# GpSimd's side jobs in the attention phase: weight sums put behind a unit's first row maxima, head sums and the power step behind the scales of every second or fourth unit

## The chip, the cores and the metric

The kernel runs on one core of one Trainium2 chip. The metric is the device time of one execution in microseconds (us). The five engines are TensorE (PE, with PEld for its weight loads), VectorE (DVE), ScalarE (ACT), GpSimd (POOL) and SyncE (SP), which here issues nearly all DMAs.

## The reference

Eight sequences of 100 latents and 361 context rows, width 1024, pass through one gated cross-attention block and one gated mixture of low-rank experts. Cut to what matters:

```python
def _L0_xattn_ref(latents, context, Wq, Wk, Wv, Wo, q_norm_w, k_norm_w):
    kv = jnp.concatenate([context, latents], axis=1)
    q = (latents @ Wq).reshape(bsz, q_len, HEADS, HEAD_DIM).transpose(0, 2, 1, 3)      # 32 heads of 128
    k = (kv @ Wk).reshape(bsz, kv_len, KV_HEADS, HEAD_DIM).transpose(0, 2, 1, 3)       # 8 KV heads
    v = (kv @ Wv).reshape(bsz, kv_len, KV_HEADS, HEAD_DIM).transpose(0, 2, 1, 3)
    q, k = rms_norm(q, q_norm_w), rms_norm(k, k_norm_w)
    scores = jnp.einsum('bhgqd,bhkd->bhgqk', q.reshape(bsz, KV_HEADS, groups, q_len, HEAD_DIM), k) * scale
    probs = jax.nn.softmax(scores.astype(jnp.float32), axis=-1)
    out = jnp.einsum('bhgqk,bhkd->bhgqd', probs, v)
    return out.transpose(...).reshape(bsz, q_len, HEADS * HEAD_DIM) @ Wo

x = x + tanh(g_xattn) * _L0_xattn_ref(layernorm(x), ctx, ...)
x = x + tanh(g_ffn) * experts(layernorm(x))        # top 2 of 8 experts of rank 16
```

## The kernel before

Every product of fp32 data is made of three fp32r matmuls (high by high, high by low, low by high). ScalarE makes a high part by a rounding copy, and VectorE makes the low part by a subtraction. The large products (keys and values, and the output projection) use seven block products in place of eight, which needs sums and differences of blocks of the weights and of the operands.

The execution has four stages: keys and values (up to about 682 us of the span), the attention of 64 units (682 to some 1441 us), the rest of the output projection, and the experts, which are partly woven into it.

**Units.** A unit u is one KV head g = u // 8 with one sequence b = u % 8, and holds R = 4 query heads. The instruction order of each engine is written out by hand in a function `slot(u)`, one for each engine. In slot u TensorE makes the four scores of unit u (`scores(u, i)`), then transposes and multiplies the probabilities of unit u - 1 (`turn_probs`, `values`), and between them makes a part of the query product for later units (`query_part`, until unit 55). I call a slot the time from TensorE's first matmul of `scores(u, 0)` (line 973, bank<-kT,q_hi) to that of unit u + 1.

**The softmax of head i of unit u.** VectorE takes the row maxima `mx` from the PSUM bank (L1923), then `nm` = -mx * rq (L1929, two operands in SBUF). ScalarE makes the exponential `pr` (L1539) with its row sum. VectorE takes the reciprocal `rr` (L1938). POOL scales `pr` by `rr` (`scale`, L901); the four scales of a unit release `turn_probs(u, 0)`. VectorE's order in a slot is: mx(0), nm(0), the low part of the previous unit's transposed probabilities `pT_lo(0)` (L1917), the query copy (L1875), mx(1), nm(1), rr(0), pT_lo(1), rr(1), mx(2), nm(2), pT_lo(2), rr(2), mx(3), nm(3), pT_lo(3), rr(3), every fourth mean square, then the next unit's `q_lo` (L1897), and in every odd slot up to 51 the low part `wq_lo` of a query weight (L1805, 128 x 1024). TensorE's `scores(u + 1, 0)` waits for `q_lo(u + 1)`, its fourth transposition in a slot for `pT_lo(1)`.

**POOL's side jobs in this phase**, all in its one in-order stream:

- `weight_sum(i)` (L912, 128 x 512, two operands in SBUF): 64 block sums of the output weights, four on each of 16 tiles `tb`. `WT_AT` says behind which unit each stands. SP loads a tile (`load_t`) two units after an earlier one's last sum (`WT_DONE`) and stores it (`store_t`) one unit after its own.
- `early_sum(n)` (L918, 128 x 400, two operands in SBUF): 16 sums S3 of finished attention heads, loaded by `load_s3` one unit ahead and stored by `store_s3` one unit later.
- `unit_rms(u)` (L896, 100 x 16 power): the factor rq for the units u to u + 3, which nm and the exponential of these units need. It waits for VectorE's mean squares.

**Buffers.** pr has two slots (unit parity), mx, nm, rs and rr one for each head i, q_hi and q_lo two, tb two, the S3 buffers four.

Of the kernel before, what the change touches and what calls it, by code (L numbers as in the profile page):

```python
# [33 lines left out]
TB = B // 2  # L34
# [94 lines left out]
UNITS = G * B  # L129
# [20 lines left out]
WT_STEPS = GQ * R  # L150
WT_AT = {}
for _n in range(4 * WT_STEPS):
    WT_AT.setdefault(max(-1, (_n - 4) * 6 // 7), []).append(_n)
WT_DONE = {n: next(u for u in WT_AT if 4 * n + 3 in WT_AT[u]) for n in range(WT_STEPS)}

S3_AT = 34
S3_STEPS = GQ * TB

UPPER = (P5, P4)
TAIL0 = FIRST_OF[P2]  # L160
# [11 lines left out]
def build(nc, x, ctxT, Wq, Wkv, Wo, AR, BmT, vecs, rows, out):  # L172
    with ExitStack() as ctx:
        def sem(name):
            return ctx.enter_context(nc.semaphore(name))
# [202 lines left out]
        mx_done = sem("mx_done")  # L378
# [90 lines left out]
        def stored(u):  # L469

            return 16 * (u // 2 + 1)
# [29 lines left out]
        def _(sp):  # L501
# [112 lines left out]
            def load_kT(u):  # L614
                g, b = u // B, u % B
                if u >= 2:
                    sp.wait_ge(s_done, 4 * (u - 2) + 4)
                r0 = b // TB * ROWS_M + b % TB * NC
                l0 = b // TB * ROWS_M + CTX_M + b % TB * NQ
                src = kT_d[:, g]  # L620
                sp.dma_start(kT[:, u % 2, :, 0:NC].bitcast(F32), src[:, :, r0:r0 + NC]).then_inc(kT_in[u % 2], 16)
                sp.dma_start(kT[:, u % 2, :, NC:NK].bitcast(F32), src[:, :, l0:l0 + NQ]).then_inc(kT_in[u % 2], 16)

            def load_vv(u):
                g, b = u // B, u % B
                if u >= 2:
                    sp.wait_ge(pv_done, u - 1)
                r0 = b // TB * ROWS_M + b % TB * NC
                l0 = b // TB * ROWS_M + CTX_M + b % TB * NQ
                dst = vv[:, u % 2].bitcast(F32)  # L630
                sp.dma_start(dst[0:ROWS[0], 0], v_d[r0:r0 + ROWS[0], g]).then_inc(vv_in[u % 2], 16)
                sp.dma_start(dst[0:ROWS[1], 1:3], v_d[r0 + OFF[1]:r0 + NC, g].rearrange("(t r) l d -> r t l d", t=2)
                             ).then_inc(vv_in[u % 2], 16)
                sp.dma_start(dst[0:NQ, 3], v_d[l0:l0 + NQ, g]).then_inc(vv_in[u % 2], 16)

            def store_attn(u):
                sp.wait_ge(ao_done, u + 1)
                sp.dma_start(at_d[u // B, u % B], ao[:, u % 2]).then_inc(ao_stored[u % 2], 16)
# [13 lines left out]
            def load_heads_of(m):  # L652
# [6 lines left out]
                if m < 2:  # L659
                    for i in range(4):  # L660
                        sp.wait_ge(s3_stored[i], 16 * S3_STEPS // 4)
                elif o in (P5, P6) and c >= 2 or m - 2 > LAST_OF[P6]:
# [27 lines left out]
            def load_chunk(m):  # L690
                load_weights(m)
                load_heads_of(m)

            def load_s3(n):
                if n >= 4:
                    sp.wait_ge(s3_stored[n % 4], 16 * (n // 4))
                for th in range(2):
                    u = n // TB * B + th * TB + n % TB
                    sp.wait_ge(ao_stored[u % 2], stored(u))
                    sp.dma_start(s3b[n % 4][th], at_d[u // B, u % B]).then_inc(s3_in[n % 4], 16)  # L700

            def store_s3(n):
                sp.wait_ge(s3_sum, n + 1)
                sp.dma_start(s3_d[n // TB, :, n % TB], s3b[n % 4][0]).then_inc(s3_stored[n % 4], 16)
# [5 lines left out]
            def load_t(n):  # L710
                if n >= 2:
                    sp.wait_ge(t_stored[n % 2], 16 * (n // 2))
                sp.dma_start(tb[:, n % 2], Wo.rearrange("n (k c) p r d -> c r p (n k) d", k=2)[n // R, n % R]).then_inc(t_in[n % 2], 16)

            def store_t(n):
                sp.wait_ge(t_sum, 4 * n + 4)
                sp.dma_start(wt_d.rearrange("t c p r d -> c r p t d")[n // R, n % R], tb[:, n % 2]).then_inc(t_stored[n % 2], 16)
# [10 lines left out]
            def load_heads(n):  # L728

                h = n // 2 + 2  # L730
                if n % 2 == 1 and 4 <= h < H:
                    load_wq(h)
# [6 lines left out]
            for u in range(UNITS):  # L739
                load_heads(u + AHEAD)  # L740
                if 1 <= u < UNITS - 1:
                    load_kT(u + 1)

                for n in range(WT_STEPS):
                    if u == WT_DONE[n] + 1:
                        store_t(n)
                    if u == WT_DONE[n] + 2 and n + 2 < WT_STEPS:
                        load_t(n + 2)
                if 0 <= u - S3_AT - 2 < S3_STEPS:
                    store_s3(u - S3_AT - 2)  # L750
                if 0 <= u - S3_AT < S3_STEPS:
                    load_s3(u - S3_AT)
                if u in (OUT0 - 2, OUT0 - 1):
                    load_chunk(u - OUT0 + 2)
                if OUT0 + 1 <= u:
                    load_chunk(u - OUT0 + 1)
                if u == UNITS - 1:
                    load_heads_of(G + 2)
                    load_heads_of(G + 3)
                if u >= 1:  # L760
                    store_attn(u - 1)
                    if u + 1 < UNITS:
                        load_vv(u + 1)
# [50 lines left out]
        def _(pool):  # L814
# [76 lines left out]
            def unit_rms(u):  # L891

                g, b = u // B, u % B
                pool.wait_ge(ms_done, 2 * g + b // TB + 1)
                c = slice(R * b, R * (b + TB))
                pool.tensor_tensor(rq[0:NQ, g, c], ms[0:NQ, c], mhalf[0:NQ, 0:R * TB], ALU.pow).then_inc(rq_done, 1)  # L896

            def scale(u, i):
                a = 4 * u + i
                pool.wait_ge(rr_done, a + 1)  # L900
                pool.tensor_scalar(pr[0:NQ, u % 2, i], pr[0:NQ, u % 2, i], rr[0:NQ, i:i + 1], None,  # L901
                                   ALU.mult).then_inc(p_done, 1)

            def weight_sum(i):

                n = i // 4
                to, a, b, minus = WT_OPS[i % 4]
                if i % 4 == 0:
                    pool.wait_ge(t_in[n % 2], 16 * (n // 2 + 1))
                elif i % 4 < 3:  # L910
                    pool.wait_ge(t_sum, i)
                pool.tensor_tensor(tb[:, n % 2, to], tb[:, n % 2, a], tb[:, n % 2, b],  # L912
                                   ALU.subtract if minus else ALU.add).then_inc(t_sum, 1)

            def early_sum(n):

                pool.wait_ge(s3_in[n % 4], 32 * (n // 4 + 1))
                pool.tensor_tensor(s3b[n % 4][0], s3b[n % 4][0], s3b[n % 4][1], ALU.subtract).then_inc(s3_sum, 1)  # L918

            def chunk_sums(m):  # L920

                o, c = CHUNKS[m]
                pool.wait_ge(at_in[m % 4], a_loaded(m))
                if o == P6:
                    pool.wait_ge(at_sum, summed(m - 1))
                to, x, y = {P5: (a21[c % 2], a21[c % 2], a22[c % 2]), P6: (a11[c % 2], a21[c % 2], a11[c % 2]),
                            P3: (at_raw[m % 2], at_raw[m % 2], at_more[:, m % 2])}[o]
                for b in range(TB):
                    pool.tensor_tensor(to[:, b], x[:, b], y[:, b], ALU.add if o == P5 else ALU.subtract).then_inc(at_sum, 1)
# [2 lines left out]
            for i in WT_AT[-1]:  # L932
                weight_sum(i)
            for u in range(UNITS):
                if u % TB == TB - 1 and u + 1 < UNITS:
                    unit_rms(u + 1)
                for i in range(R):
                    scale(u, i)
                for i in WT_AT.get(u, ()):
                    weight_sum(i)  # L940
                if 0 <= u - S3_AT - 1 < S3_STEPS:
                    early_sum(u - S3_AT - 1)
                if u == UNITS - 2:
                    chunk_sums(FIRST_OF[P5])
            for m in range(FIRST_OF[P6], LAST_OF[P6] + 1):
# [1249 lines left out]
```

## Time and profile before

| | |
|---|---|
| median of 3 runs | 1715.55 us (1714.4 to 1715.92) |
| the profiled execution: its time, and its span | 1715.65 us, 1713.8 us |
| busy over the span: PE, PEld, DVE, ACT, POOL | 97%, 86%, 72%, 50%, 51% |
| busy from 900 to 1100 us (200 us): PE, DVE, ACT, POOL | 199.06, 155.84, 119.46, 143.14 us |
| busy from 1100 to 1300 us: PE, DVE, ACT, POOL | 198.01, 155.13, 119.85, 160.93 us |
| granted TensorE clock in these two stretches | 1.00 |

PE counts as busy while a matmul is in its pipeline, so a short wait between two matmuls need not show as idle time; the starts of the same matmul in successive slots show it. Times in the rows are us from the start of the span, durations behind "x" counts are those of the merged group.

### The profile page before, as it was taken

To read this page: it belongs to the slowest core of one execution; us is meant where nothing else is said; L and a number is where in the kernel's file an instruction comes from. 1 tells how busy PE (TensorE), PEld (TensorE's weight loads), DVE (VectorE), ACT (ScalarE), POOL (GpSimd) and SP (SyncE) were. 2 spreads that over 40 slices of the span, in tenths; PEclk is the share of its full clock that TensorE was granted. 3 is DMA by queue.
4 is the path that set the end of the run, shared out by engine and by line. 5 is a ranking of instruction groups with operands and counts; after the bars stand their busy time and mean duration, and the time that the engine had idled before them with its cause. 6 is when DMAs were issued, how large, how long until landed. Compare 5 with 4: busy or idle time off the path is not lost.

```text
span 1713.8 us, 26112 instructions
## 1 busy us (share of the span) xinstructions
PE 1665.8 (97%) x9120; PEld 1475.3 (86%) x9120; DVE 1239.6 (72%) x2078; ACT 865.1 (50%) x1647; POOL 873.9 (51%) x668
## 2 busy tenths in 40 slices
PE   7999999999999999999999999999999999999996
PEld 6788888678888869899999999999999889999994
DVE  7788776677777742777777777777776876557767
ACT  5445554454444432555666565665555666443321
POOL 1454444134443320766767667788786445543320
PEclk9999999999999999999999999999999999999998
DMA  5667778636666564456555554666756557676632
GB/s 196 161 181 233 235 210 241 183 108 186 162 184 154 140 239 150 138 159 191 188 156 187 182 179 160 213 217 216 232 181 215 170 205 267 212 275 229 241 116 68
DMA packets 238502, 323.86 MB, mean 189 GB/s; under 512 B 53300, under 2 KB 193396, under 8 KB 233380
## 3 DMA queue, kind: packets, MB, share of 16 engines
q1 hardware_dynamic: 237796, 315.65, 59.8%
q10 hardware_dynamic: 576, 6.55, 0.9%
q8 instruction: 73, 1.20, 0.3%
q14 instruction: 57, 0.47, 0.1%
HBM read 212.18 MB, written 109.97 MB: 188 GB/s over the span
## 4 chain that ended last, share of the span: by engine, by line
PE 70%; DVE 18%; issue 4%; ACT 4%; DMA 2%; POOL 0%; DVEq 0%; SPq 0%; ACTq 0%; POOLq 0%
PE bank L973 21%; PE bank L975 20%; PE bank L974 20%; DVE mx L1923 4%; PE bank L1111 3%; DVE wq_lo L1805 3%; DVE q_lo L1897 3%; PE bank L1078 2%; DVE pT_lo L1917 2%; DMA kT_d<-kst 1%; PE bank L1007 1%; ACT pr L1539 1%; DVE q_raw L1875 1%; DVE nm L1929 1%; DVE wo_lo L1943 1%
## 5 line engine op out<-in xcount | busy, mean ns | idle before, releaser
L901 POOL TENSOR_SCALAR pr<-pr,rr 100x461 f32<-100x461 f32 x256 | 370.2, 1454 | 231.6 <-DVE rr L1938 231.6
L973 PE MATMUL bank<-w_hi,a_hi 128*128 128x512 f32 (+1 forms) x856 | 340.8, 398 | 11.7 <-DVE a_lo L1713 8.6
L975 PE MATMUL bank<-w_hi,a_lo 128*128 128x512 f32 (+1 forms) x856 | 334.8, 391 | 0.0
L974 PE MATMUL bank<-w_lo,a_hi 128*128 128x512 f32 (+1 forms) x856 | 334.3, 390 | 0.0
L1539 ACT ACTIVATE pr<-bank,nm,rq 100x461 f32<-100x461 f32 x256 | 188.8, 737 | 187.6 <-DVE nm L1929 186.2
L855 POOL TENSOR_TENSOR msk<-ssk,epst 128x4 f32<-128x4 f32 (+1 forms) x60 | 23.5, 391 | 348.5 <-DVE ssk L1744 348.5
L973 PEld LDWEIGHTS bank<-w_hi,a_hi 128*128 128x128 f32 (+1 forms) x856 | 157.8, 184 | 48.8 <-issue 9.7
L1923 DVE TENSOR_REDUCE mx<-bank 100x1 f32<-100x461 f32 x256 | 160.6, 627 | 48.7 <-PE bank L975 47.2
L975 PEld LDWEIGHTS bank<-w_hi,a_lo 128*128 128x128 f32 (+1 forms) x856 | 157.5, 184 | 38.0
L973 PE MATMUL bank<-xT_hi,wq_hi 128*128 128x400 f32 x512 | 188.9, 369 | 0.5 <-issue 0.5
L974 PEld LDWEIGHTS bank<-w_lo,a_hi 128*128 128x128 f32 (+1 forms) x856 | 158.0, 185 | 34.8
L975 PE MATMUL bank<-xT_hi,wq_lo 128*128 128x400 f32 x512 | 178.3, 348 | 0.0
L974 PE MATMUL bank<-xT_lo,wq_hi 128*128 128x400 f32 x512 | 178.2, 348 | 0.0
L973 PE MATMUL bank<-at_hi,wo_hi 128*128 128x400 f32 x448 | 159.9, 357 | 2.9 <-DVE at_lo L1954 2.5
L974 PE MATMUL bank<-at_lo,wo_hi 128*128 128x400 f32 x448 | 155.7, 347 | 0.0
L975 PE MATMUL bank<-at_hi,wo_lo 128*128 128x400 f32 x448 | 155.6, 347 | 0.0
L1530 ACT ACTIVATE pT_hi<-bank 120x400 fp32r<-120x400 f32 (+2 forms) x256 | 127.6, 498 | 52.2 <-PE bank L1111 51.4
L1917 DVE TENSOR_TENSOR pT_lo<-bank,pT_hi 120x400 fp32r<-120x400 f32 (+2 forms) x256 | 144.5, 565 | 8.0 <-ACT pT_hi L1530 7.6
L1111 PEld LDWEIGHTS bank<-ident,pr 100*120 100x120 f32 (+2 forms) x1024 | 111.1, 149 | 19.5 <-DVE pT_lo L1917 7.2
L1111 PE MATMUL bank<-ident,pr 100*120 100x100 f32 (+2 forms) x1024 | 122.3, 255 | 2.3 <-DVE pT_lo L1917 0.4
L1713 DVE TENSOR_TENSOR a_lo<-st,a_hi 128x512 fp32r<-128x512 f32 (+1 forms) x104 | 91.5, 881 | 34.8 <-ACT a_hi L1332 34.8
L1332 ACT ACTIVATE a_hi<-st 128x512 fp32r<-128x512 f32 (+1 forms) x104 | 63.2, 609 | 83.8 <-PE bank L975 73.6
(154 smaller groups left out, 3635.1 us busy)
## 6 DMA issues: line engine op xcount, KB each, us to landing
kT_d<-kst SPq DMA_DIRECT2D x56, 512.0 KB, 5.7
v_d<-vst SPq DMA_DIRECT2D x56, 512.0 KB
kT<-kT_d SPq DMA_DIRECT2D x64, 361.0 KB, 4.5
kvr<-ctxT SPq DMA_DIRECT2D x44, 512.0 KB, 6.2
wq_raw<-Wq SPq DMA_DIRECT2D x32, 512.0 KB, 5.8
tb<-Wo SPq DMA_DIRECT2D x16, 1024.0 KB, 8.3
wt_d<-tb SPq DMA_DIRECT2D x16, 1024.0 KB, 8.0
wo_raw<-wt_d SPq DMA_DIRECT2D x16, 1024.0 KB, 7.4
```

Source lines behind the costliest of these rows:

```text
L901: pool.tensor_scalar(pr[0:NQ, u % 2, i], pr[0:NQ, u % 2, i], rr[0:NQ, i:i + 1], None, ALU.mult).then_inc(p_done, 1)
L973: pe.matmul(o, lh, rh, start=start, stop=False, skip_group_check=more)
L974: pe.matmul(o, lh, rl, start=False, stop=False, skip_group_check=more)
L975: return pe.matmul(o, ll, rh, start=False, stop=stop, skip_group_check=more)
L1111: mm = pe.transpose(ps[ptbank(u, t)][0:ROWS[t], i * NQ:(i + 1) * NQ], pr[0:NQ, u % 2, i, OFF[t]:OFF[t] + ROWS[t]], ident[0:NQ, 0:NQ])
L1332: act.activation(a_hi[:, i % RING, :, 0:cols(k % NT)], a_src(i), ACT.Copy).then_inc(a_hi_done, 1)
L1530: act.activation(pT_hi[0:ROWS[t], t], ps[ptbank(u, t)][0:ROWS[t], 0:QW], ACT.Copy).then_inc(pT_hi_done, 1)
L1539: act.activation(pr[0:NQ, u % 2, i], ps[BS[i % 2]][0:NQ, 0:NK], ACT.Exp, bias=nm[0:NQ, i:i + 1], scale=rq[0:NQ, g, R * b + i:R * b + i + 1 ...
L1713: dve.tensor_tensor(a_lo[:, i % RING, :, 0:n], a_src(i), a_hi[:, i % RING, :, 0:n], ALU.subtract).then_inc(a_lo_done, 1)
L1805: dve.tensor_tensor(wq_lo[:, h % 2], wq_raw[:, h % 2], wq_hi[:, h % 2], ALU.subtract).then_inc(wq_lo_done, 1)
L1917: dve.tensor_tensor(pT_lo[0:ROWS[t], t], ps[ptbank(u, t)][0:ROWS[t], 0:QW], pT_hi[0:ROWS[t], t], ALU.subtract).then_inc(pT_lo_done, 1)
L1923: dve.tensor_reduce(mx[0:NQ, i:i + 1], ps[BS[i % 2]][0:NQ, 0:NK], AX.X, ALU.max).then_inc(mx_done, 1)
```

## The change

Three things move, all in POOL's stream or in what SP does for it; no operation is added or removed.

1. The 64 weight sums stand ahead of a unit's scales instead of behind them, and wait for the unit's first maxima (`mx_done` of 4u + 1). Their units are one higher: -1: 3 sums, unit 0: 1, and then one or two sums for each of the units 1 to 51 (two in the units 1, 7, 13, 19, 25, 31, 37, 43, 49). SP's stores and loads of the tiles follow one unit later.
2. The power for the units u + 2 to u + 5 stands behind the scales of unit u with u % 4 = 2; before, it stood ahead of the scales of the next unit, behind the weight sum (and the S3 sum) of unit u.
3. The 16 S3 sums stand behind the scales of the units 20, 22, ..., 50 (loads 19, 21, ..., 49, stores 21, 23, ..., 51); before, behind those and the weight sums of the units 35 to 50.

```diff
 for _n in range(4 * WT_STEPS):
-    WT_AT.setdefault(max(-1, (_n - 4) * 6 // 7), []).append(_n)
+    WT_AT.setdefault(max(-1, (_n - 4) * 6 // 7 + 1), []).append(_n)
 
-S3_AT = 34
 S3_STEPS = GQ * TB
+S3_AT = [19 + 2 * n for n in range(S3_STEPS)]
...
-                if 0 <= u - S3_AT - 2 < S3_STEPS:
-                    store_s3(u - S3_AT - 2)
-                if 0 <= u - S3_AT < S3_STEPS:
-                    load_s3(u - S3_AT)
+                if u - 2 in S3_AT:
+                    store_s3(S3_AT.index(u - 2))
+                if u in S3_AT:
+                    load_s3(S3_AT.index(u))
...
             for u in range(UNITS):
-                if u % TB == TB - 1 and u + 1 < UNITS:
-                    unit_rms(u + 1)
+
+                if u in WT_AT:
+                    pool.wait_ge(mx_done, 4 * u + 1)
+                for i in WT_AT.get(u, ()):
+                    weight_sum(i)
                 for i in range(R):
                     scale(u, i)
-                for i in WT_AT.get(u, ()):
-                    weight_sum(i)
-                if 0 <= u - S3_AT - 1 < S3_STEPS:
-                    early_sum(u - S3_AT - 1)
+                if u % TB == TB - 2 and u + 2 < UNITS:
+                    unit_rms(u + 2)
+                if u - 1 in S3_AT:
+                    early_sum(S3_AT.index(u - 1))
```

## Rows read from the trace of the kernel before

**Rows 1.** The page's first part: busy us, share, instructions.
```profile
PE 1665.8 (97%) x9120; PEld 1475.3 (86%) x9120; DVE 1239.6 (72%) x2078; ACT 865.1 (50%) x1647; POOL 873.9 (51%) x668
```

**Rows 2.** Timeline, PE: start, duration; first score matmul of units 2, 29, 30, 31, 52, 53.
```profile
709.78 0.37 PE L973 MATMUL bank<-kT,q_hi 128*100 128x462 f32 x1
...
1023.62 0.38 PE L973 MATMUL bank<-kT,q_hi 128*100 128x462 f32 x1
...
1034.99 0.37 PE L973 MATMUL bank<-kT,q_hi 128*100 128x462 f32 x1
...
1046.81 0.38 PE L973 MATMUL bank<-kT,q_hi 128*100 128x462 f32 x1
...
1292.65 0.37 PE L973 MATMUL bank<-kT,q_hi 128*100 128x462 f32 x1
...
1304.00 0.38 PE L973 MATMUL bank<-kT,q_hi 128*100 128x462 f32 x1
```

**Rows 3.** Timeline, POOL and DVE, end of slot 29, into slot 30.
```profile
1032.82 1.44 POOL L901 TENSOR_SCALAR pr<-pr,rr 100x461 f32<-100x461 f32 x1 [0.61 <-DVE rr L1938]
1032.99 1.58 DVE L1897 TENSOR_TENSOR q_lo<-q_raw,q_hi 128x400 fp32r<-128x400 f32 x1 [0.26 <-ACT q_hi L1519]
1034.23 1.49 POOL L912 TENSOR_TENSOR tb<-tb 128x512 f32<-128x512 f32 x1
1034.49 2.31 DVE L1805 TENSOR_TENSOR wq_lo<-wq_raw,wq_hi 128x1024 fp32r<-128x1024 f32 x1
```

**Rows 4.** Timeline, DVE, end of slot 51 (no weight sum here) and start of 52.
```profile
1290.81 0.90 DVE L1897 TENSOR_TENSOR q_lo<-q_raw,q_hi 128x400 fp32r<-128x400 f32 x1 [0.26 <-ACT q_hi L1519]
1291.75 1.23 DVE L1805 TENSOR_TENSOR wq_lo<-wq_raw,wq_hi 128x1024 fp32r<-128x1024 f32 x1
1293.48 0.64 DVE L1923 TENSOR_REDUCE mx<-bank 100x1 f32<-100x461 f32 x1 [0.50 <-PE bank L975]
```

**Rows 5.** Timeline, three engines, inside slot 29; the last row is from slot 30.
```profile
1024.46 0.64 DVE L1923 TENSOR_REDUCE mx<-bank 100x1 f32<-100x461 f32 x1 [1.26 <-PE bank L975]
...
1025.24 0.16 DVE L1929 SCALAR_TENSOR_TENSOR nm<-mx,rq 100x1 f32<-100x1 f32 x1
...
1027.17 0.16 DVE L1929 SCALAR_TENSOR_TENSOR nm<-mx,rq 100x1 f32<-100x1 f32 x1
1027.27 0.16 DVE L1938 RECIPROCAL rr<-rs 100x1 f32<-100x1 f32 x1
1027.35 0.56 DVE L1917 TENSOR_TENSOR pT_lo<-bank,pT_hi 120x400 fp32r<-120x400 f32 x1
...
1027.53 2.87 POOL L901 TENSOR_SCALAR pr<-pr,rr 100x461 f32<-100x461 f32 x2 [3.19 <-DVE rr L1938]
...
1028.63 0.79 PE L1078 MATMUL bank<-ones,sq 128*100 128x2 f32 x8
...
1039.48 0.56 DVE L1917 TENSOR_TENSOR pT_lo<-bank,pT_hi 120x400 fp32r<-120x400 f32 x1
...
1040.47 0.79 PE L1078 MATMUL bank<-ones,sq 128*100 128x2 f32 x8
```

**Rows 6.** Timeline, POOL and DVE: nm beside weight sums, and nm beside the power.
```profile
684.96 5.24 POOL L912 TENSOR_TENSOR tb<-tb 128x512 f32<-128x512 f32 x4
...
689.25 0.97 DVE L1929 SCALAR_TENSOR_TENSOR nm<-mx,rq 100x1 f32<-100x1 f32 x1
...
1190.59 0.16 DVE L1929 SCALAR_TENSOR_TENSOR nm<-mx,rq 100x1 f32<-100x1 f32 x1
```

**Rows 7.** Timeline, PE and POOL: slot 43 and the start of slot 44.
```profile
1186.76 0.38 PE L973 MATMUL bank<-kT,q_hi 128*100 128x462 f32 x1
...
1188.92 1.05 POOL L918 TENSOR_TENSOR at_raw<-at_raw 128x400 f32<-128x400 f32 x1
1189.94 2.93 POOL L896 TENSOR_TENSOR rq<-ms,mhalf 100x16 f32<-100x16 f32 x1
1192.87 5.71 POOL L901 TENSOR_SCALAR pr<-pr,rr 100x461 f32<-100x461 f32 x4
...
1198.95 0.43 PE L973 MATMUL bank<-kT,q_hi 128*100 128x462 f32 x1 [0.63 <-issue]
```

## The prediction

> **What bounds the kernel now.** I read the page's busy shares first: TensorE is busy for 1665.8 of 1713.8 us [rows 1]. No other engine comes near, so a change on POOL can only return time that TensorE spends waiting. The list of waits between 700 and 1300 us gives TensorE almost none. That list is no proof, since a matmul waiting in the pipeline still counts as busy. So I then took, from the timeline, TensorE's first score matmul of each unit, and compared the slots. This shows what the busy share hides [rows 2]:
>
> - Slot 29 takes 1034.99 - 1023.62 = 11.37 us, slot 30 takes 1046.81 - 1034.99 = 11.82 us, and slot 52 takes 1304.00 - 1292.65 = 11.35 us. TensorE's instructions are the same in all three. Odd slots are at 11.37, even ones at 11.82 as long as there are weight sums, and an even slot without them is at 11.35.
> - The 50 slots 2 to 51 take 1292.65 - 709.78 = 582.87 us. At the undisturbed lengths they would take 25 x 11.37 + 25 x 11.35 = 568.0 us. So 14.9 us are lost here. That is the most that the change can return in this stage.
>
> **Where the 0.45 us of an even slot go.** The timeline at the end of an odd slot shows it. The weight sum starts right behind the fourth scale, and VectorE's q_lo (two operands in SBUF) takes 1.58 us and wq_lo 2.31 us; wq_lo ends 1.81 us into slot 30 [rows 3]. At the end of slot 51, with the scale but no weight sum, they take 0.90 and 1.23 us, wq_lo ends 0.33 us into slot 52, and VectorE then waits for TensorE's scores [rows 4]. So the weight sum costs VectorE 0.68 + 1.08 = 1.76 us, after which it is late in the even slot: pT_lo(1) ends 5.05 us into slot 30 (1039.48 + 0.56 - 1034.99) against 4.29 us into slot 29, 0.76 us later, and TensorE's squares, which stand behind the transposition that needs it, start 5.48 us in against 5.01, 0.47 us later [rows 2, 5]. So VectorE may be late by 0.76 - 0.47 = 0.29 us at pT_lo(1), and each further us is one on the path.
>
> **Part 1, the weight sums.** Behind the fourth scale nothing reads or writes `tb` any more, so the ends of the odd slots become those of slot 51 [rows 4]: q_lo 0.90, wq_lo 1.23 us. The 25 even slots go to 11.35, the odd ones keep 11.37.
>
> The sum now starts when mx(0) is done. POOL is idle there: a unit's scales start 1027.53 - 1023.62 = 3.91 us into a slot, mx(0) ends 1.48 us in, and one sum takes 1.31 (5.24 for four) to 1.49 us [rows 3, 5, 6]. So a single sum is over 1.6 + 1.3 = 2.9 us into the slot, before the scales and before nm(1) at 3.55 us [rows 5]. The work of VectorE between nm(0) and nm(1) (pT_lo, the query copy, mx(1)) has a PSUM operand. What the sum does meet is nm, with two SBUF operands. Row 689.25 shows the price: nm was issued 0.36 us into the last of four weight sums and took 0.97 us, until 690.22, where that sum ended [rows 6]. So nm is held until a sum's end, 1.33 us after its start.
>
> For nm(0) it is a tie. It starts 0.14 us after mx(0) ends; POOL starts a scale 0.10 us after the rr that releases it (1027.43 to 1027.53), with one wait, where the sum has two [rows 5]. From both sides: nm(0) costs nothing more if it gets in first, and 1.33 - 0.14 = 1.2 us if not. I take nothing: the two starts are within 0.04 us and nm is a single short read. The other end is the first rival.
>
> Double sums do meet nm(1). In the units 13, 25, 37 and 49 the second runs from 2.9 to 4.2 us; nm(1), due at 3.55 to 3.71, ends at 4.24, 0.53 late. Less the 0.29 of slack that is 0.24 us on the path, x 4 = 1.0 us.
>
> **Part 2, the power.** It takes 2.93 us [rows 7] and goes from behind the sums of unit u to right behind its scales. A slot's last scale ends 0.73 us ahead of the next slot (1032.82 + 1.44 against 1034.99) [rows 2, 3], so the power runs to 2.2 us into the slots 3, 7, ..., 51, 13 slots. It does not hold nm: at 1190.59, 0.65 us into a power, nm took its 0.16 us [rows 6, 7]. But it pushes the weight sum of those slots behind it. In 3, 11 and 15 the sum runs from 2.2 to 3.5 us, just ahead of nm(1): no cost. In 7 and 19 the second sum runs from 3.5 to 4.8 us; nm(1) comes 0.05 us after its start and either gets in (0) or is 1.1 us late (0.8 on the path). I take half, 2 x 0.4 = 0.8 us. The scales there start at 4.8 instead of 3.9, which the gaps between them absorb.
>
> The Trainium skill (SBUF — State Buffer, "SBUF: two separate sides") says that the port pair which GpSimd shares with VectorE is an exclusive lock that the first comer holds for its whole instruction. The weight sum's row agrees; the power's row does not. By the rule the power's new place would also hold nm(0) in 13 slots, from 1.6 to 2.2 us, for 13 x (0.6 - 0.29) = 4.0 us more; the measured rows decide.
>
> **Part 3, the S3 sums.** One takes 1.05 us when it has no wq_lo beside it [rows 7]. They go behind the scales of even units, where no wq_lo follows, and take the place of the weight sum that q_lo has beside it now; the odd slots bear that at 11.37. Where no power stands between (n even) this costs nothing. Behind the power (units 22, 26, ..., 50) power and S3 sum end at 2.2 + 1.05 = 3.2 us, and the weight sum runs from there to 4.55, over nm(1), which ends at 4.55 instead of 3.71: 0.84 late, 0.55 on the path. In the six slots 23, 27, 35, 39, 47, 51 with one sum that is 3.3 us. In 31 and 43, with two, the scales start at 3.2 + 2.6 = 5.8 us. Slot 43 shows what this costs today: two weight sums, S3 sum and power put its scales at 1192.87 - 1186.76 = 6.11 us, they run without a gap to 11.82 us, and the slot takes 12.19 us, 0.82 too long [rows 2, 7]. With nm(1) held as well (0.55) I take 1.3 us each, 2.6 us. What slot 43 pays now is inside the 14.9.
>
> **SP and the ends.** The tile stores and loads go one unit later, the sums by some 3 us only, so a tile keeps about 2.5 slots (28 us) from its load to its first sum, and in the list of waits POOL waits for no DMA in this stage. The last tile store is at unit 52, two units ahead of its use; the last S3 store stays at 51. The S3 loads come every second unit instead of each. None of these is waited for. In the slots 0 and 1, POOL still has four weight sums ahead of the first scales; and from slot 52 on its stream is the same.
>
> **The sum.** 14.9 returned, less 1.0 + 0.8 + 3.3 + 2.6 = 7.7 us, is 7.2 us gained: 1715.65 - 7.2 = 1708.4 us for the profiled execution. The median is 0.10 lower (1715.55); I forecast 1708.4 us.
>
> **Rivals.**
>
> - *The sum takes the port ahead of nm(0).* Then nm(0), pT_lo(0), the query copy, mx(1), nm(1) and pT_lo(1) all come 1.2 us late, 0.9 us on the path, in the 37 slots of 2 to 51 in which mx(0) and not the power releases the sum: 33 us against the gain of 7, so some 1742 us. It decides from 8 such slots on. For it: the two are released by the same event, and rr to scale (0.10 us) is quicker than mx to nm (0.14). Against: the sum's second wait, and nm's single element. Chance 0.16. By the page's rule named above (the first to start gets the pair for its whole instruction) this tie is decided by hundredths of a us, either way.
> - *No change.* The losses behind power and S3 sum are as large as the gain (the double sums of 7, 19, 31, 43 at 2 us each, the six at 0.84, the four at 0.53, 15 us), so that time stays within 3.4 us of before: 1713 to 1716 us. Chance 0.10.
> - *All of it comes back.* nm(1) slips in between, or TensorE has slack there that slot 30 does not show: 14.9 us, 1700.8 us. Chance 0.12.
> - *The forecast*, losses between a half and 1.4 of mine: 1704.5 to 1711.5 us. Chance 0.62.
>
> **The numbers.** 0.2% is 3.4 us, about what a measurement of this kernel can tell from no change. Faster 0.74, same 0.10, slower 0.16. The range reaches from the third case to the top of the second with a margin: 1701 to 1717 us; that leaves out the first rival alone. The forecast's own is 1704.5 to 1711.5.
>
> **What would show it.** Right: wq_lo at 1.23 us, even slots at 11.35, all nm(0) at 0.16 us, and nm(1) around 1 us in the slots 23, 27, 35, 39, 47, 51. Wrong at part 1: nm(0) at 1.3 us in slots such as 4 and 5, and slots of 12.2 us. Wrong at part 3: slots 23, 27 and so on at 11.4. Also wrong if wq_lo stays at 2.3 us, or if SP stands at a store and the key loads come late.

## The result, and the profile after

The changed kernel takes 1745.85 us (median of 4 runs, 1745.02 to 1746.99) against 1714.97 us before: a ratio of 1.0181 (95% interval 1.0163 to 1.0199). It is 31 us slower. The forecast was 1708.4 us; its first rival, with a chance of 0.16, stood at 1742 us.

The page's first line shows little of it: TensorE is busy for 16 us more, and its share falls only from 97 to 96% [rows 1].

```profile
PE 1681.7 (96%) x9120; PEld 1475.7 (85%) x9120; DVE 1245.5 (71%) x2078; ACT 862.5 (49%) x1647; POOL 859.1 (49%) x668
```

The list of waits of the changed kernel from 700 to 1330 us (total us, times, longest) names both ends of the new chain: POOL's sums released by the maxima 37 times, and TensorE (its weight loads and its matmuls) waiting for pT_lo. Before, from 700 to 1300 us, these two rows of TensorE had 8.2 us in 25 times and 0.6 us in three.

```profile
POOL tb L912 <- DVE mx L1926: 74.8, 37, 3.0
...
PEld bank L976 <- DVE pT_lo L1920: 31.0, 50, 2.3
...
PE bank L976 <- DVE pT_lo L1920: 10.7, 13, 2.0
```

In TensorE's timeline (start, duration) the first score matmuls of the units 2 and 52 answer to [rows 2].

```profile
709.73 0.37 PE L976 MATMUL bank<-kT,q_hi 128*100 128x462 f32 x1
...
1323.59 0.37 PE L976 MATMUL bank<-kT,q_hi 128*100 128x462 f32 x1
```

The 50 slots take 613.86 us, against 582.87 before. That is 31.0 us, and the span grew by 30.9 (1713.8 to 1744.7). All of the loss lies in these slots. The timeline of slot 4 (a slot without a power ahead), for three engines:

```profile
734.41 0.37 PE L976 MATMUL bank<-kT,q_hi 128*100 128x462 f32 x1
...
735.23 0.64 DVE L1926 TENSOR_REDUCE mx<-bank 100x1 f32<-100x461 f32 x1 [0.65 <-PE bank L978]
735.95 1.30 POOL L912 TENSOR_TENSOR tb<-tb 128x512 f32<-128x512 f32 x1 [2.27 <-DVE mx L1926]
736.00 1.26 DVE L1932 SCALAR_TENSOR_TENSOR nm<-mx,rq 100x1 f32<-100x1 f32 x1
...
737.18 0.56 DVE L1920 TENSOR_TENSOR pT_lo<-bank,pT_hi 121x400 fp32r<-121x400 f32 x1
...
738.87 0.16 DVE L1932 SCALAR_TENSOR_TENSOR nm<-mx,rq 100x1 f32<-100x1 f32 x1
...
746.41 0.38 PE L976 MATMUL bank<-kT,q_hi 128*100 128x462 f32 x1
```

The gain that was forecast is there: mx(0) comes 0.82 us into the even slot, so VectorE is no longer late at its start. But the weight sum starts 0.08 us after mx(0) ends (735.87 to 735.95) and nm(0) 0.05 us later. nm(0) takes 1.26 us instead of 0.16, to the end of the sum. nm(1) then comes 4.46 us into the slot, where it comes at 3.52 when nothing holds nm(0) (experiment 1 below), and the slot takes 12.00 us.

In the slots behind a power it is worse, and slot 27 shows how: nm(0) is issued while the power runs, and is held through the rest of the power and the S3 sum.

```profile
1017.20 2.95 POOL L896 TENSOR_TENSOR rq<-ms,mhalf 100x16 f32<-100x16 f32 x1
1017.85 0.38 PE L976 MATMUL bank<-kT,q_hi 128*100 128x462 f32 x1
...
1018.69 0.64 DVE L1926 TENSOR_REDUCE mx<-bank 100x1 f32<-100x461 f32 x1 [1.34 <-PE bank L978]
1019.46 1.72 DVE L1932 SCALAR_TENSOR_TENSOR nm<-mx,rq 100x1 f32<-100x1 f32 x1
...
1020.12 1.05 POOL L918 TENSOR_TENSOR at_raw<-at_raw 128x400 f32<-128x400 f32 x1
...
1021.13 1.28 POOL L912 TENSOR_TENSOR tb<-tb 128x512 f32<-128x512 f32 x1
```

Slot 7, with a power and two sums, is the longest, 16.77 us (770.44 to 787.21). nm(0) is held for 3.13 us, to the end of both sums, and TensorE stands for 1.97 us. In the windows (PE, PEld, DVE, ACT, POOL busy, granted clock, DMA share, GB/s) the granted clock falls behind this stop: to 0.50, the lower of its two levels (1.2 GHz), from 776.92 to 783.74 us.

```profile
772.06 3.13 DVE L1932 SCALAR_TENSOR_TENSOR nm<-mx,rq 100x1 f32<-100x1 f32 x1
...
772.68 2.50 POOL L912 TENSOR_TENSOR tb<-tb 128x512 f32<-128x512 f32 x2
...
775.73 0.46 PE L976 MATMUL bank<-pT_hi,vv 121*128 121x400 f32 x1 [1.97 <-DVE pT_lo L1920]
```

```profile
778.00:787.21 9.21, 9.21 (x42) 8.86 (x41) 5.03 (x12) 4.43 (x9) 4.93 (x4) 0.69 0.00 0
787.21:799.21 12.00, 11.83 (x74) 10.71 (x72) 8.32 (x18) 6.43 (x15) 7.04 (x5) 1.00 0.73 227
```

### The profile page after: what moved, and what is told of

Its sections match the earlier page's. It is cut to its first block, busy times and chain, and to the rows that moved or that the text cites. A ratio compares the mean times of both kernels' runs of the same rounds, so it can differ in the third digit from the quotient of the medians.

```text
span 1744.7 us, 26150 instructions
## 1 busy us (share of the span) xinstructions
PE 1681.7 (96%) x9120; PEld 1475.7 (85%) x9120; DVE 1245.5 (71%) x2078; ACT 862.5 (49%) x1647; POOL 859.1 (49%) x668
## 4 chain that ended last, share of the span: by engine, by line
PE 73%; DVE 15%; issue 6%; ACT 3%; POOL 1%; DMA 0%; DVEq 0%; SPq 0%; ACTq 0%; POOLq 0%
PE bank L976 22%; PE bank L978 21%; PE bank L977 21%; DVE mx L1926 4%; DVE pT_lo L1920 4%; PE bank L1114 2%; PE bank L1081 2%; PE bank L1010 1%; DVE q_raw L1878 1%; DVE wo_lo L1946 1%; PE bank L1293 1%; DVE at_lo L1948 1%; ACT pr L1542 1%; DVE nm L1932 1%; ACT w_hi L1358 1%
## 5 line engine op out<-in xcount | busy, mean ns | idle before, releaser
L1932 DVE SCALAR_TENSOR_TENSOR nm<-mx,rq 100x1 f32<-100x1 f32 x256 | 125.0, 488 | 29.0 <-DVE mx L1926 0.9
L1114 PE MATMUL bank<-ident,pr 100*120 100x100 f32 (+2 forms) x1024 | 127.3, 256 | 5.8 <-DVE pT_lo L1920 1.3
L912 POOL TENSOR_TENSOR tb<-tb 128x512 f32<-128x512 f32 x64 | 82.2, 1287 | 75.3 <-DVE mx L1926 74.8
```

The lines of the kernel that those rows point to most:

```text
L1114: mm = pe.transpose(ps[ptbank(u, t)][0:ROWS[t], i * NQ:(i + 1) * NQ], pr[0:NQ, u % 2, i, OFF[t]:OFF[t] + ROWS[t]], ident[0:NQ, 0:NQ])
L1932: dve.scalar_tensor_tensor(out=nm[0:NQ, i:i + 1], in0=mx[0:NQ, i:i + 1], scalar=-1.0, in1=rq[0:NQ, g, R * b + i:R * b + i + 1], op0=ALU.mu ...
```

## The experiments

Two theories stood against each other. **The port:** a weight sum of POOL and VectorE's nm (two operands in SBUF) exclude one another, and the sum starts first. **The place:** the sums, the power or the S3 sums cost by being early in the slot, next to pT_lo, the query copy and the maxima, or behind the scales.

The ratio is to the kernel before as it was timed together with that run (medians 1714.97, 1715.71 and 1717.63 us); the slots are those of the profiled execution.

| run | median us | ratio to before, 95% interval | slots 2 to 51, us |
|---|---|---|---|
| before | 1714.97 | | 582.87 |
| the change | 1745.85 | 1.0181 (1.0163 to 1.0199) | 613.86 |
| sums wait for nm(0) | 1709.19 | 0.9954 (0.9937 to 0.9971) | 575.45 |
| parts 1 and 2, S3 sums as before | 1750.41 | 1.0197 (1.0180 to 1.0214) | 615.78 |
| part 3 (S3 sums) alone | 1714.08 | 0.9988 (0.9979 to 0.9998) | 580.83 |
| one fill ahead of the sum | 1748.87 | 1.0194 (1.0174 to 1.0214) | 612.56 |
| four fills ahead of the sum | 1709.17 | 0.9954 (0.9940 to 0.9968) | 577.74 |
| sums between nm and nm | 1701.22 | 0.9914 (0.9901 to 0.9928) | 568.52 |
| no wait behind a power | 1729.53 | 1.0073 (1.0057 to 1.0090) | 596.53 |
| nm(0), S3 sums as before | 1709.38 | 0.9955 (0.9941 to 0.9969) | 575.30 |

**1. The sum waits for nm(0) instead of mx(0).**

```diff
-                    pool.wait_ge(mx_done, 4 * u + 1)
+                    pool.wait_ge(nm_done, 4 * u + 1)
```

> The changed kernel, but the weight sum waits for the unit's first nm (the sum cannot then reach the port ahead of it). If the held nm(0) is the cause of the loss, nm(0) takes 0.16 us again in all slots and the time comes to my first forecast of some 1708 us (1704 to 1712); the slots that follow a power, where nm(0) was held through power and sum, lose their hold too, since POOL then waits and has no sum queued behind the power. If the loss comes from the sum being early in the slot at all (its overlap with pT_lo, the query copy and the maxima), or from the power and the S3 sums, the time stays above 1735 us.

Measured: 1709.19 us, with one word changed. Slot 4 in this run's timeline:

```profile
732.78 0.37 PE L976 MATMUL bank<-kT,q_hi 128*100 128x462 f32 x1
...
734.38 0.16 DVE L1932 SCALAR_TENSOR_TENSOR nm<-mx,rq 100x1 f32<-100x1 f32 x1
...
734.62 1.29 POOL L912 TENSOR_TENSOR tb<-tb 128x512 f32<-128x512 f32 x1 [2.60 <-DVE nm L1932]
...
736.30 0.16 DVE L1932 SCALAR_TENSOR_TENSOR nm<-mx,rq 100x1 f32<-100x1 f32 x1
...
744.13 0.38 PE L976 MATMUL bank<-kT,q_hi 128*100 128x462 f32 x1
```

The sum runs next to pT_lo, the query copy and mx(1), as it does in the changed kernel, and costs nothing: the slot takes 11.35 us. nm(0) is at 0.16 us in all slots, those behind a power too. The theory of the place falls for these neighbours. What is left over the floor of 568 us is 7.4 us, and it lies in the 14 slots where a sum runs over nm(1), as here in slot 23:

```profile
952.82 1.07 POOL L918 TENSOR_TENSOR at_raw<-at_raw 128x400 f32<-128x400 f32 x1
...
953.86 1.28 POOL L912 TENSOR_TENSOR tb<-tb 128x512 f32<-128x512 f32 x1
...
954.17 0.99 DVE L1932 SCALAR_TENSOR_TENSOR nm<-mx,rq 100x1 f32<-100x1 f32 x1
```

**2. Parts 1 and 2 without part 3.** The changed kernel with the S3 sums in their old units. The power stays in its new place, behind the scales and ahead of the next unit's weight sum, so this run does not part the weight sums from the power; experiments 1 and 6 do.

```diff
-S3_AT = [19 + 2 * n for n in range(S3_STEPS)]
+S3_AT = [34 + n for n in range(S3_STEPS)]
```

> The weight sums' move alone (part 1): S3 sums in the units 35 to 50 as before. If part 1 alone carries the loss, 1742 to 1750 us, the time of the whole change within some 4 us. If the S3 sums or the power behind the scales carry it, within 10 us of before.

Measured: 1750.41 us. The S3 sums' new places have no share in the loss. Even slots are at 12.0 us up to slot 34. From 36 on most take 12.4 to 12.5, since an S3 sum behind an odd unit's scales makes q_lo 1.35 and wq_lo 2.1 us. Slots 7 and 31, with nm(0) held for 3.15 us and TensorE standing for 1.99 us, take 13.92 us each here, without a fall of the clock.

**3. The S3 sums' move alone**, on the kernel before.

```diff
-S3_AT = 34
 S3_STEPS = GQ * TB
+S3_AT = [19 + 2 * n for n in range(S3_STEPS)]
```

> The S3 sums' move alone on the kernel before (part 3; weight sums behind the scales, power ahead of the scales of every fourth unit). By the slots of before, 43, 44 and 46 lose some 0.4 to 0.8 us each to piled POOL work and would be relieved, while slot 31 would get such a pile: within 2 us of before. If part 3 is what costs, over 1720 us.

Measured: 1714.08 us, 0.12% below before, at the edge of what can be told. Slot 43 takes 11.52 us instead of 12.19 and slot 44 11.40 instead of 12.18; slot 31 did not get the pile that I expected (11.39).

**4 and 5. Fills of 128x1 between the wait and the sum**, one and then four, to move the sum's start by hundredths of a us. The fills write a tile that nothing reads.

```diff
                     pool.wait_ge(mx_done, 4 * u + 1)
+                    for j in range(4):
+                        pool.memset(pad[:, 4 * u + j:4 * u + j + 1], 0.0)
```

> The changed kernel with one tiny POOL fill (128x1) between the wait for the first maxima and the weight sum, which puts the sum's start some tenths of a us later and leaves everything else. If the loss is decided by who of sum and nm(0) starts first, nm(0) takes 0.16 us in the 37 slots without a power ahead, these slots go to about 11.35 us, and the time falls to 1710 to 1722 us (the 13 slots behind a power may keep their 1.1 to 1.4 us each). If it is not a matter of the first start, nm(0) stays at 1.2 us or is held for the rest of the sum, and the time stays near 1746 us.

> The changed kernel with four tiny POOL fills between the wait for the first maxima and the sum. With one fill the sum still started 0.02 us ahead of nm(0) and nm(0) took 1.29 us. Four should put the sum some 0.1 to 0.2 us behind nm(0)'s start. If the first start decides, nm(0) takes 0.16 us in the 37 slots without a power ahead, and the time is 1710 to 1722 us. If what decides is something else (the sum already waiting in POOL's queue, or the fills themselves), nm(0) stays above 1 us and the time near 1747 us.

Measured: with one fill 1748.87 us, with four 1709.17. The timeline of slot 5 with one fill, and then with four:

```profile
748.53 0.10 POOL L939 MEMSET pad<- 128x1 f32 x1 [2.18 <-DVE mx L1928]
748.59 1.29 POOL L913 TENSOR_TENSOR tb<-tb 128x512 f32<-128x512 f32 x1
748.61 1.29 DVE L1934 SCALAR_TENSOR_TENSOR nm<-mx,rq 100x1 f32<-100x1 f32 x1
```

```profile
747.34 0.19 POOL L940 MEMSET pad<- 128x1 f32 x4 [2.27 <-DVE mx L1929]
747.42 0.16 DVE L1935 SCALAR_TENSOR_TENSOR nm<-mx,rq 100x1 f32<-100x1 f32 x1
747.49 1.29 POOL L913 TENSOR_TENSOR tb<-tb 128x512 f32<-128x512 f32 x1
```

One fill was too little: the sum is still 0.02 us ahead, and nm(0) takes 1.29 us. With four it starts 0.07 us behind nm(0), which takes 0.16 us. So the order of the two starts decides, and the medians lie 40 us apart. In the profiled executions the 50 slots differ by 34.8 us: 24.3 us in the 37 slots where 0.09 us in the sum's start is what changed, and 10.6 us in the 13 behind a power. (The profiled execution with four fills was the slowest of six, at 1714.04 us. In its slot 31, nm(1) was held for 2.32 us over both sums, TensorE stood for 1.62 us, the granted clock was 0.50 from 1052.59 to 1056.00 us, and the slot took 14.74 us.)

My lower bound of 1710 us was a little too high, because the slots behind a power lost their hold as well. Slot 3 with four fills:

```profile
722.30 2.93 POOL L897 TENSOR_TENSOR rq<-ms,mhalf 100x16 f32<-100x16 f32 x1
...
724.68 0.16 DVE L1935 SCALAR_TENSOR_TENSOR nm<-mx,rq 100x1 f32<-100x1 f32 x1
...
725.18 0.19 POOL L940 MEMSET pad<- 128x1 f32 x4
725.32 1.30 POOL L913 TENSOR_TENSOR tb<-tb 128x512 f32<-128x512 f32 x1
```

Here too the maxima let the fills and the sum go while the power runs, and yet nm(0) takes 0.16 us. With one fill it took 1.96 us in this slot. So four fills do more here than move a start, and what, is not shown. In the 37 other slots experiment 1 answers that doubt: it has no fills, its sums start behind nm(0) too, and nm(0) takes the same 0.16 us.

**6. What holds nm(0) behind a power.** In the units 3, 7, ..., 51 the sum waits for nothing.

```diff
-                if u in WT_AT:
+                if u in WT_AT and u % TB != TB - 1:
                     pool.wait_ge(mx_done, 4 * u + 1)
```

> The changed kernel, but in the units 3, 7, ..., 51 (behind a power) the sum waits for nothing, so it stands in POOL's queue from the start of the slot; in the changed kernel nm(0) is held there from 1.62 us through the rest of the power and the sum behind it (1.9 us, in slots 7 and 31 over 2.9). If a sum that waits in the queue behind the running power holds nm, these slots stay as they are, 12.5 to 12.7 us, and the time stays within 2 us of 1746 us. If it is the moment at which the maxima release the sum, just ahead of nm(0), that takes the port, nm(0) takes 0.16 us in these 13 slots and the time falls by 13 times 1.0 to 1.3 us, to 1729 to 1733 us.

Measured: 1729.53 us. Slot 3 of this run:

```profile
719.82 3.18 POOL L896 TENSOR_TENSOR rq<-ms,mhalf 100x16 f32<-100x16 f32 x1
...
722.11 0.16 DVE L1932 SCALAR_TENSOR_TENSOR nm<-mx,rq 100x1 f32<-100x1 f32 x1
...
722.97 1.28 POOL L912 TENSOR_TENSOR tb<-tb 128x512 f32<-128x512 f32 x1
```

nm(0) is issued in the running power, with the sum behind it in the stream, and takes 0.16 us. The same nm took 1.9 us in the changed kernel, where the maxima released the sum just before nm(0). So neither the power nor a sum queued behind it holds nm. It is held where the maxima release the sum while the power runs, with nothing, one fill or an S3 sum between power and sum; with four fills between, the same release did not hold it (experiment 5, slot 3). nm(0) takes 0.16 us in 12 of the 13 slots and 0.28 in slot 31; nm(1) is held in the 8 with an S3 sum, which stay at 11.9 us. The power itself takes 3.18 us here instead of 2.93; why is not shown.

**7. Between nm and nm.** Every sum waits for an nm: one for nm(0), a second one, and the one behind power and S3 sum, for nm(1). Doubles stand in the units 5, 9, 13 and so on, never behind a power.

```diff
+WT_PLACES = [-1] * 4 + [_u for _u in range(1, 64) for _ in range(2 if _u % 4 == 1 and _u > 1 else 1)]
...
+                for j, i in enumerate(WT_AT.get(u, ())):
+                    behind = 2 if j == 1 or u % TB == TB - 1 and u - 2 in S3_AT else 1
+                    pool.wait_ge(nm_done, 4 * u + behind)
+                    weight_sum(i)
```

> A version planned from the rows: each weight sum waits for an nm, one sum for nm(0) (1.86 to 3.15 us into the slot), a unit's second one, and the one behind a power with S3 sum, for nm(1) (3.7 to 5.0 us); doubles stand in the units 5, 9, 13, ... only. Power and S3 sums as in the change. With only nm(0) waited for, the slots with a sum over nm(1) still took 11.87 in place of 11.38 us. If nm is all that a sum costs, all 50 slots take 11.35 to 11.4 us and the time is 1701 to 1704 us. If scales that start 1.0 us late also cost, or the sum over rr(0) and pT_lo(1), 1706 us or more.

Measured: 1701.22 us, the fastest version, 0.9914 of before. Slot 5, with two sums, and the ends of the 50 slots:

```profile
744.22 1.29 POOL L913 TENSOR_TENSOR tb<-tb 128x512 f32<-128x512 f32 x1 [2.58 <-DVE nm L1933]
...
745.91 0.16 DVE L1933 SCALAR_TENSOR_TENSOR nm<-mx,rq 100x1 f32<-100x1 f32 x1
...
746.14 1.28 POOL L913 TENSOR_TENSOR tb<-tb 128x512 f32<-128x512 f32 x1 [0.63 <-DVE nm L1933]
...
747.40 5.71 POOL L902 TENSOR_SCALAR pr<-pr,rr 100x461 f32<-100x461 f32 x4
```

```profile
708.27 0.37 PE L977 MATMUL bank<-kT,q_hi 128*100 128x462 f32 x1
...
1276.79 0.37 PE L977 MATMUL bank<-kT,q_hi 128*100 128x462 f32 x1
```

They take 568.52 us, within 0.5 us of the floor. The scales start 5.0 us into the slot instead of 3.9, run without a gap, and nobody waits for them.

**8. nm(0), with the S3 sums of before.** Experiment 1 with the edit of experiment 2.

> The weight sums released by nm(0), with the S3 sums of before (units 35 to 50, each unit). Against the run with nm(0) and the new S3 places (1709.2 us) this shows what part 3 is worth once part 1 works. S3 sums behind odd units' scales bring back q_lo and wq_lo at 1.35 and 2.1 us, as the run with the weight sums alone showed, which made the even slots 42 to 50 some 0.5 us longer: 8 x 0.4 us = 3 us, less the S3 sums that no longer push sums over nm(1) in 23, 27 and 31 (1.5 us): 1710 to 1713 us. If only part 3's spread made that run fast, over 1715 us.

Measured: 1709.38 us, no different from experiment 1 (0.9955 and 0.9954 of their befores). Slot 46 is 0.3 us longer, but only four slots with an S3 sum in front push their weight sum over nm(1), where eight do with the new places. Part 3 is worth nothing here; I had expected 1 to 4 us.

## Why the prediction was wrong

- **What bounds, and where the 0.45 us of an even slot go: right.** With nm left alone, even slots take 11.35 us and wq_lo 1.23 us. Nearly all of the 14.9 us of the stage can be had: experiment 7 has 14.35 of them (582.87 - 568.52), and experiment 1 lands by the 1708.4 us that I forecast for the change, at 1709.19.
- **The failed step is "For nm(0) it is a tie. ... I take nothing".** I took the cheap end of a bound of 0 to 1.2 us, 37 times over, because the sum's second wait and nm's small size spoke for nm. Neither did anything: in all 37 slots the sum starts 0.08 us after mx(0) ends and nm(0) 0.13, and nm(0) takes 1.25 us or more. Experiments 4 and 5 show that the order of these two starts decides, and that 0.02 us are enough for the sum. This step alone turned the gain into a loss: 24 us, against 7.2 forecast as gain.
- **The rival's size.** I put the 37 slots at 0.9 us on the path each. They take 12.00 and 12.03 us, 0.65 too long, together 24 us. The late pT_lo(1) explains it by the slack of 0.29 us that the even slots gave: nm(0) ends 1.10 us late, not 1.2, the instructions behind it follow one another more closely, so nm(1) comes 0.94 late, and 0.94 - 0.29 = 0.65. That this rival's 1742 us lies near the measured 1745.85 is luck: it priced the 37 slots too high and left out the 13 behind a power.
- **Part 2, "It does not hold nm", was right of the power and wrong of its slot.** I looked for what the power does to nm, and then let the sum start at 2.2 us, "no cost" in 3, 11 and 15. But the maxima release the sum while the power runs, and nm(0) is held from then on. The 13 slots lie together 21.6 us above 11.37: 169.4 us in place of 147.8. Of that, some 2.9 us are slot 7's, where the granted clock fell behind a stop of 1.97 us (16.77 us against 13.92 in experiment 2, with the same hold and no fall).
- **The losses at nm(1): right in their sum, in part by luck.** I had 7.7 us, and experiment 1 shows 7.4, but errors of the shares cancel. The double sums of 13, 25, 37 and 49 cost 0.4 to 0.5 us each (0.24 forecast), because the sums wait for nm(0) there and the second ends at 4.4 to 4.5 us instead of 4.2. 7 and 19 cost 0.7 and 0.8 (0.4): nm(1) never got in ahead of the second sum. The slots with S3 sum and one weight sum cost 0.5 (0.55), and 31 and 43 only 0.5 (1.3), since nm(1) gets in between the two weight sums. In the changed kernel itself nm(1) comes so late that of these losses only slot 43's shows (nm(1) 0.98 us).
- **Part 3 and SP: no loss.** With nm(0) free there is no gain either (experiments 1 and 8). In the changed kernel part 3 gives back 3.9 us in the even slots: they lie 16.3 us over their floor, and 20.2 in experiment 2.

The account of the 31.0 us: before, the slots had 14.9 us over the floor. After, they have 16.3 (25 even slots), 7.9 (12 odd ones without a power) and 21.6 (13 behind one), 45.9 in all (613.86 - 568.0).

The Trainium skill (SBUF — State Buffer, "SBUF: two separate sides") says of a GpSimd operation that reads SBUF and a VectorE operation with two SBUF inputs that whichever starts first gets the shared pair for the whole instruction. For the weight sum experiments 4 and 5 agree, to 0.02 us. For the power the runs do not: nm(0) took 0.16 us inside it in experiment 6. And behind a power in the changed kernel nm(0) was held from 1.62 us into slot 3 on, though the sum started only at 2.24 us.

## What to carry to other kernels

Work that is moved to where its engine is idle must be asked which short instruction of the other engine is released by the same event. If both want the same port, the order of two starts hundredths of a us apart decides, here the same way in all 37 slots, so a tie is to be removed by a wait on the short one's result and never to be priced at its cheap end. A bound that is multiplied by 37 belongs on the side of caution, and the slots' lengths from the starts of one recurring matmul show what busy shares and lists of waits hide.

## What the runs showed of the hardware that I had not expected

- A two-input sum on POOL (128x512, 1.3 us) that starts 0.02 us ahead of VectorE's 100x1 operation with two SBUF inputs holds it for 1.29 us. One that starts 0.07 us behind it does not hold it at all.
- POOL answered to the maxima in 0.08 us, with one or two waits ahead of the sum, quicker than VectorE to its own result with three (0.13 us).
- A sum released while POOL was still in the power held nm from the moment of nm's issue: to the end of the sum (1.9 us in slot 3), to the end of both sums (3.13 us in slot 7, but only 1.93 us in slot 19), or to the end of an S3 sum in between (1.72 us in slot 27). A sum with nothing to wait for, queued behind the same power, did not, and neither did one with four fills in front. What POOL does at the release is not shown by any run here; that stays open.
- Slots 7 and 19 differ by one wait of the kernel. In `weight_sum`, the second sum of slot 19 waits for the first one's result and starts 0.08 us after it ends (3.53 to 3.61 us into the slot), and nm(0) ends in this gap. The second sum of slot 7 has no such wait and starts 0.05 us before the first ends, and nm(0) is held over both; so it is in slot 31 of experiment 2. In experiment 5 nm(1) fares alike: it is held over both sums in slot 31 (2.32 us, no wait between them), and over the first alone in slot 43 (1.05 us, with the wait). The gap is not all of it: in the slots 13 and 37 of the changed kernel the second sum starts without one, and nm(0) still ends with the first. The rows of slot 19:

```profile
922.26 1.93 DVE L1932 SCALAR_TENSOR_TENSOR nm<-mx,rq 100x1 f32<-100x1 f32 x1
...
922.89 2.64 POOL L912 TENSOR_TENSOR tb<-tb 128x512 f32<-128x512 f32 x2
```

- One stop of TensorE of 1.97 us was followed by a stretch at a mean granted clock of 0.69, in which 128x400 matmuls took up to 0.54 us instead of 0.35, some 2.9 us lost. In experiment 5 a stop of 1.62 us was followed by one too. The two stops of 1.99 us in experiment 2, those of 2.02 and 1.83 us in experiment 4, and the one of 1.79 us in slot 31 of the changed kernel were not, so the length of the stop alone does not tell.
